# A decoder layer on one core: the causal mask of the maximum as TensorE matmuls, one VectorE reduction over two banks, and a bank of its own for rope

## The reference

```python
# attention: 16 heads of 8, keys and values from a normalised 32-wide latent, rope on q and k, causal
q = (x @ W_q).reshape(b, t, 16, 8).transpose(0, 2, 1, 3)
lat = layernorm(x @ W_dkv) * gamma + beta
k, v = heads(lat @ W_uk), heads(lat @ W_uv)
scores = einsum("bhqd,bhkd->bhqk", rope(q), rope(k)) / sqrt(8)
attn = softmax(where(causal, scores, -inf))
x = x + (attn @ v).reshape(b, t, 128) @ W_o
# cross-attention over 32 context rows: 8 heads of 64, softmax, output projection and bias
# feed-forward 128 -> 352 -> 128: silu(gate) * up, with inputs and weights of every product
# rounded to FP4 in blocks of 16 (scale = max(abs) / 6)
```

## Time and profile before

| | before |
|---|---|
| median of 3 runs, us | 447.8 (447.5 to 450.05) |
| profiled execution, own time / its span, us | 448.12 / 446.4 |
| mean granted clock | 0.75 |
| TensorE busy (matmul) | 300.2 us, 67% |
| VectorE busy | 306.3 us, 69% |
| ScalarE busy | 173.5 us, 39% |
| GpSimd busy | 201.2 us, 45% |
| L821, fused maximum, 256 of them | 114.3 us busy, 49.9 idle before |
| L1069, fills, 256 matmuls | 43.5 us busy, 69.0 idle before |

### The profile page before, as it was taken

How to read it: one execution, slowest core, us unless ns; L and a number is a source line. 1 busy time by engine, 2 the same in 40 slices (tenths; PEclk the granted TensorE clock), 3 DMA queues, 4 the chain that set the end, 5 groups by cost and what they waited for, 6 DMA issues and landing times.

```text
span 446.4 us, 6519 instructions
## 1 busy us (share of the span) xinstructions
PE 300.2 (67%) x1790; PEld 145.2 (33%) x1790; DVE 306.3 (69%) x1136; ACT 173.5 (39%) x326; POOL 201.2 (45%) x376
## 2 busy tenths in 40 slices
PE   0441475877876867869877768596968847567464
PEld 0220142323223222224443324244333314345243
DVE  5742876665575567677788787878778554786972
ACT  1140154565545465243545443444435423222210
POOL 8400033742133444444475644445354661745563
PEclk9995555768788579575969686778859679865796
DMA  6019400025030034003002320030000000000000
GB/s 179 0 61 224 118 0 1 3 100 117 0 73 1 2 121 95 0 1 78 1 8 71 100 50 7 1 76 2 9 1 7 8 1 7 6 1 7 1 12 18
DMA packets 20836, 17.50 MB, mean 39 GB/s; under 512 B 1921, under 2 KB 20225, under 8 KB 20801
## 3 DMA queue, kind: packets, MB, share of 16 engines
q1 hardware_dynamic: 20272, 16.50, 14.8%
q10 hardware_dynamic: 528, 0.59, 0.4%
HBM read 9.62 MB, written 7.34 MB: 38 GB/s over the span
## 4 chain that ended last, share of the span: by engine, by line
PE 45%; DVE 27%; issue 10%; ACT 6%; POOL 6%; DMA 3%; SPq 1%; POOLq 0%; DVEq 0%; ACTq 0%
PE pvp L1104 10%; PE mxp L1069 6%; DVE summed L821 5%; PE st L1093 5%; PE misc L1183 3%; ACT probs L624 2%; PE pvp L1115 2%; PE misc L1165 2%; DVE space L755 2%; PE misc L1168 2%; PE misc L1140 2%; DVE space L752 2%; POOL space L461 2%; DVE xn L735 2%; PE mxp L1004 2%
## 5 line engine op out<-in xcount | busy, mean ns | idle before, releaser
L821 DVE CUSTOM_DVE_ANT_0 summed<-mxp,causal 128x512 bf16<-128x512 f32 (+3 forms) x256 | 114.3, 485 | 49.9 <-PE mxp L1069 49.0
L624 ACT ACTIVATE probs<-st 128x1024 f32<-128x1024 f32 (+1 forms) x96 | 84.5, 880 | 115.6 <-PE st L1093 115.4
L1069 PE MATMUL mxp<-ks,qs 48*128 48x512 bf16 (+3 forms) x256 | 43.5, 377 | 69.0 <-DVE rmax L821 50.4
L1104 PE MATMUL pvp<-probs,va 128*32 128x128 f32 (+3 forms) x512 | 62.5, 565 | 5.1 <-POOL probs L431 5.1
L431 POOL TENSOR_SCALAR_AFFINE_SELECT probs<-probs 128x256 f32<-128x256 f32 x128 | 48.0, 411 | 33.0 <-ACT probs L624 33.0
L1093 PE MATMUL st<-qs,ks 50*128 50x512 bf16 (+3 forms) x256 | 42.3, 371 | 8.2 <-ACT probs L624 6.2
L1069 PEld LDWEIGHTS mxp<-ks,qs 48*128 48x128 bf16 x256 | 12.2, 99 | 92.8 <-DVE rmax L821 44.5
L534 ACT ACTIVATE space<-misc 128x128 f32<-128x128 f32 (+3 forms) x78 | 24.2, 327 | 39.6 <-PE misc L1124 20.2
L422 POOL TENSOR_SCALAR var<-mv 128x1 f32<-128x1 f32 (+1 forms) x36 | 8.9, 248 | 56.9 <-DVE mv L728 55.6
L1093 PEld LDWEIGHTS st<-qs,ks 50*128 50x128 bf16 x256 | 12.1, 101 | 62.4 <-issue 41.5
L461 POOL TENSOR_TENSOR space<-space 128x128 f32<-128x128 f32 (+2 forms) x33 | 24.7, 747 | 15.3 <-DVE space L758 15.3
(11 more groups left out here) (196 smaller groups left out, 587.8 us busy)
## 6 DMA issues: line engine op xcount, KB each, us to landing
parts_dram<-parts SPq DMA_DIRECT2D x8, 384.0 KB, 2.6
qs<-parts_dram SPq DMA_DIRECT2D x16, 192.0 KB, 3.8
ks<-parts_dram SPq DMA_DIRECT2D x16, 192.0 KB, 4.2
parts_dram<-parts SPq DMA_DIRECT2D x8, 256.0 KB, 2.9
xin<-in_x SPq DMA_DIRECT2D x4, 256.0 KB, 6.0
parts_dram<-parts SPq DMA_DIRECT2D x8, 128.0 KB, 2.7
out<-outr SPq DMA_DIRECT2D x16, 64.0 KB, 1.5
qs<-nrows SPq DMA_DIRECT2D x32, 4.0 KB
```

The source lines that it names most:

```text
L624: nc.scalar.activation(probs[n % 2][:, 2 * pair:2 * pair + 2, 512 * k:512 * k + w], st2[:, :].rearrange("p (h q) -> p h q", h=2)[:, :, 0:w ...
L821: last = v.tensor_tensor_reduce(out=summed[:, m % 2, e * w:(e + 1) * w], in0=mxp[m % 3][:, e * w:(e + 1) * w], in1=causal[:, S - w:S], sca ...
L1069: last = mm(units[r][:, e * w:(e + 1) * w], qs[rows, c, i * P:(i + 1) * P], ks[rows, c, 0:w], start=True, stop=True)
L1104: last = mm(pvp[32 * i:32 * i + 32, j * P:S], va[:, j, GH * (n % NG) + i, :], probs[n % 2][:, i, OFF[j]:OFF[j] + S - P * j], start=(j == 0 ...
```

## The change

Six larger units take the place of twelve. TensorE puts the unit of row half 0 into bank 4 and that of row half 1 into bank 5, and then adds the causal mask of the diagonal tile into the same banks by matmuls: for the two halves `lo` of the 128 queries, the 64-row identity strip times the mask strip, with the accumulation left open by the score matmul. The mask's lower half needs only its last 64 columns. One tensor_reduce with negate=True reads both banks (up to 1024 elements per partition) and gives the negative maximum of 2 or 4 rows, so the rows of ks are +1 and not -1. Fill and reduction steps are moved; rope, projections, values_in and set-up use bank 6 (`side`, formerly the third bank of the maxima); the transposed rows of maxima use bank 1 (formerly bank 6). In what the diff leaves out, ScalarE and VectorE read `side` where they read misc[0] or banks[MX_BANK] for xnT, lat, latT, va, rope and set-up, TensorE claims SIDE_BANK for the same pieces, VectorE's loop runs over six units, and ScalarE copies the bank to `halves` ahead of its first piece.

```diff
-MX_BANK, PV_BANK = 4, 7
+MX_BANK, SIDE_BANK, PV_BANK = 4, 6, 7
-MAX_STEPS = [((0, 3), (0, 4)), ((0, 5),), ((0, 6),), ((0, 7), (0, 8)), ((0, 9),), ((0, 10), (0, 11)), (), (),
-             ((1, 0), (1, 1)), ((1, 2),)]
-PAIR_STEPS = [((0, 2),), (), ((0, 3),), ((0, 4),), (), ((0, 5),), (), (), ((1, 0),), ((1, 1),)]
+MAX_STEPS = [(0, 2), None, (0, 3), (0, 4), None, (0, 5), None, (1, 0), None, (1, 1)]
+FILL_STEPS = [(0, 2), (0, 3), None, (0, 4), (0, 5), None, (1, 0), None, (1, 1), None]
-MAX_UNITS = [(3, 0, 0, 1), (3, 1, 0, 1), (3, 0, 1, 1), (3, 1, 1, 1), (2, 0, 0, 1), (2, 1, 0, 1), (2, 0, 1, 1),
-             (2, 1, 1, 1), (1, 0, 0, 2), (1, 1, 0, 2), (0, 0, 0, 2), (0, 1, 0, 2)]
+MAX_UNITS = [(3, 0, 1), (3, 1, 1), (2, 0, 1), (2, 1, 1), (1, 0, 2), (0, 0, 2)]
+NUNIT = len(MAX_UNITS)
...
-        mxp = [pb(f"mxp{i}") for i in range(3)]
+        mx2 = pb("mx2", 1024)
+        mxp = [mx2[:, 0:512], mx2[:, 512:1024]]
         pvp = pb("pvp")
-        misc = [pb(f"misc{i}") for i in range(2)]
-        banks = misc + stp + mxp + [pvp]
+        misc = [pb(f"misc{i}") for i in range(3)]
+        side = misc[2]
+        banks = misc[0:2] + stp + mxp + [side, pvp]
...
-            g.memset(ks[32:HALF, :, :], -1.0)
-            g.memset(ks[HALF + 32:P, :, :], -1.0).then_inc(s["consts_ready"], 1)
+            g.memset(ks[32:HALF, :, :], 1.0)
+            g.memset(ks[HALF + 32:P, :, :], 1.0).then_inc(s["consts_ready"], 1)
...
             def max_rows(n):
                 act.wait_ge(s["nrows_mm"], n + 1)
                 wait(act, "nrows_placed", 32 * n)
-                copy(nrows[:, :], banks[MX_BANK + 2][0:2 * GH, 0:S // 2].bitcast(bf16)).then_inc(s["nrows_d"], 1)
+                copy(nrows[:, :], misc[1][0:2 * GH, 0:S // 2].bitcast(bf16)).then_inc(s["nrows_d"], 1)
...
-                wait(dve, "rmax_d", 12 * n + m - 1)
-                for e in range(k):
-                    last = v.tensor_tensor_reduce(out=summed[:, m % 2, e * w:(e + 1) * w],
-                                                  in0=mxp[m % 3][:, e * w:(e + 1) * w], in1=causal[:, S - w:S],
-                                                  scale=1.0, scalar=NEG, op0=ALU.add, op1=ALU.max,
-                                                  accum_out=rmax[:, i, r, c + e:c + e + 1])
-                last.then_inc(s["rmax_d"], 1)
+                both = mx2[:, :].rearrange("p (r q) -> p r q", r=2)[:, :, 0:k * w]
+                v.tensor_reduce(nmax[:, i, :, c:c + k], both.rearrange("p r (e w) -> p r e w", e=k), axis=AX.X,
+                                op=ALU.max, negate=True).then_inc(s["nmax_d"], 1)
...
-            def max_pair(n, p):
+            def max_fill(n, m):
...
-                units = [claim(MX_BANK + m % 3, "rmax_d", 12 * n + m + 1) for m in (2 * p, 2 * p + 1)]
+                claim(MX_BANK, "nmax_d", NUNIT * n + m + 1)
+                claim(MX_BANK + 1, "nmax_d", NUNIT * n + m + 1)
                 for e in range(k):
                     c = GH // 2 * g + c0 + e
                     for r in range(2):
                         rows = slice(HALF * r, HALF * r + SPLIT)
-                        last = mm(units[r][:, e * w:(e + 1) * w], qs[rows, c, i * P:(i + 1) * P], ks[rows, c, 0:w],
-                                  start=True, stop=True)
-                        if e == k - 1:
-                            last.then_inc(s["mx_mm"], 1)
+                        mm(mxp[r][:, e * w:(e + 1) * w], qs[rows, c, i * P:(i + 1) * P], ks[rows, c, 0:w],
+                           start=True, stop=False)
+                    for lo in range(2):
+                        for r in range(2):
+                            rows = slice(HALF * r, HALF * r + HALF)
+                            last = mm(mxp[r][:, e * w + i * P + HALF * lo:(e + 1) * w], halves[rows, lo, 0:P],
+                                      halves[rows, lo, P + HALF * lo:2 * P], start=False, stop=(lo == 1))
+                last.then_inc(s["mx_mm"], 1)
...
-                m = claim(MX_BANK + 2, "nrows_d", n + 1)[0:2 * GH, 0:S // 2].bitcast(bf16)
+                m = claim(1, "nrows_d", n + 1)[0:2 * GH, 0:S // 2].bitcast(bf16)
...
             pe.wait_ge(s["consts_ready"], 2)
+            m = claim(SIDE_BANK, "halves_d", 1)
+            for lo in range(2):
+                pick = identb[:, HALF * lo:HALF * lo + HALF]
+                for r in range(2):
+                    last = mm(m[HALF * r:HALF * r + HALF, 2 * P * lo:2 * P * lo + 2 * P], pick, squares[:, :],
+                              start=True, stop=True)
+            last.then_inc(s["halves_mm"], 1)
...
-            for p in range(6):
-                max_pair(0, p)
+            for m in range(NUNIT):
+                max_fill(0, m)
             max_rows(0)
-            for p in range(2):
-                max_pair(1, p)
+            for m in range(2):
+                max_fill(1, m)
```

More of the change, by code:

```diff
@@ L414, in _ @@
                                 pattern=[[-1, P]], channel_multiplier=1)
-            g.affine_select(out=causal[:, S - P:S], in_=causal[:, S - P:S], compare_op=ALU.is_ge, fill=NEG, base=0,
+            g.affine_select(out=causal[:, :], in_=causal[:, :], compare_op=ALU.is_ge, fill=NEG, base=0,
                             pattern=[[-1, P]], channel_multiplier=1)
@@ L563, in project @@
                     wait(act, "v_mm", b)
-                    nc.scalar.activation(latT[0:LAT, :], misc[0][0:LAT, :], ACT.Identity, bias=beta[:, :],
+                    nc.scalar.activation(latT[0:LAT, :], side[0:LAT, :], ACT.Identity, bias=beta[:, :],
                                          scale=gamma[:, :]).then_inc(s["latT_d"], 1)
[L566 to L572, removed]
+                for which in range(2):
+                    if (g, u) == WHEN[f"swap{which}"]:
+                        act.wait_ge(s["cos_d"], 2 * b + which + 1)
+                        wait(act, "low_d", 2 * b + which - 1)
+                        copy(turned[0:P // 2, which, 1, :], side[P // 2:P, :])
+                        copy(turned[P // 2:P, which, 1, :], side[0:P // 2, :]).then_inc(s["swapped_d"], 1)
                 if (g, u) == WHEN["high0"]:
@@ L687, in _ @@
             act.wait_ge(s["consts_ready"], 2)
+            act.wait_ge(s["halves_mm"], 1)
+            copy(halves[:, :, :].rearrange("p e q -> p (e q)"), side[:, :]).then_inc(s["halves_d"], 1)
             for name in ("xnT", "lat", "swap0", "latT", "high0", "swap1", "mid0", "high1", "mid1"):
@@ L758, in round_fp4, with turn_cos @@
                 v.scalar_tensor_tensor(norm, norm, BIT_DOWN, expo, ALU.mult, ALU.add).then_inc(s[sum_name], 1)
-            def turn_cos(b, side):
-                n = 2 * b + side
+            def turn_cos(b, which):
+                n = 2 * b + which
                 dve.wait_ge(s["rope_mm"], n + 1)
                 wait(dve, "low_d", n - 1)
-                v.tensor_tensor(turned[:, side, 0, :], banks[MX_BANK][:, :], cos[:, :], ALU.mult)\
+                v.tensor_tensor(turned[:, which, 0, :], side[:, :], cos[:, :], ALU.mult)\
                     .then_inc(s["cos_d"], 1)
@@ L960, in _ @@
                         set_up(n, u)
-                    for ahead, m in MAX_STEPS[u]:
-                        if in_range(n + 1 + ahead):
-                            max_unit(n + 1 + ahead, m)
+                    if MAX_STEPS[u] and in_range(n + 1 + MAX_STEPS[u][0]):
+                        max_unit(n + 1 + MAX_STEPS[u][0], MAX_STEPS[u][1])
         @block.tensor
@@ L1215, in _ @@
                         set_up(SET_UP.index((n, u)))
-                    for ahead, p in PAIR_STEPS[u]:
-                        if in_range(n + 1 + ahead):
-                            max_pair(n + 1 + ahead, p)
+                    if FILL_STEPS[u] and in_range(n + 1 + FILL_STEPS[u][0]):
+                        max_fill(n + 1 + FILL_STEPS[u][0], FILL_STEPS[u][1])
                     if in_range(n - 1):
```

48 lines of the change are left out of this document (23 added, 25 removed).

## The result

The changed kernel takes 473.1 us (median of 4 runs, 471.8 to 475.2) against 448.1 before: a ratio of 1.056, interval 1.050 to 1.061, so +25 us where +16.4 was forecast. Medians are over all runs of a kernel, ratios and their intervals leave out those that came out slow (in a slower state or over 1.5% above the kernel's fastest), so the two can differ a little.

The account below looks back on a forecast made before the run. No engine is full; TensorE and VectorE hand work back and forth, so the chain bounds the kernel. Start 3.5, late slots 10, light slots 2.5 and side bank 0.4 add 16.4 us to 448.1: 464.5 us, range 450 to 478.

Parts of the forecast that it names:

- Start: Before the loop, six fills and reductions no longer overlap: 11.8 us instead of 8.3, +3.5 us.
- VectorE's work: Per slot, plain reductions cost 6.2 us against 6.6 for the fused instructions: a gain of 0.4 us.
- Masks: TensorE's mask matmuls: eight blocks per slot, 0.11 us each at full clock and 0.16 at half, 0.9 to 1.3 us.
- Late slots: Slots 5 to 14: +1.0 us each along the chain, bounds -0.3 to +2.3, together +10 us.
- Step (e): Late slot: fill (0, 5), now at u4, waits for reduction (0, 4), +0.2 us, and its own masks +0.2.
- rival 1: Denser TensorE work keeps the granted clock up in late slots: -3.0 us per slot, 434.5 us if all ten; chance 0.11.
- Light slots: Slots 0 to 4, where scores and exponentials alternate: +0.5 us each, +2.5 together, bounds 0 and +1.5 each.
- (b): Behind L746, reduction (1, 1) takes 1.22 us where one of 0.62 + 0.09 released the fill before: +0.5 us.
- (c): The masks of fills (0, 2) and (0, 3) run at half clock on the path: +0.3 us.
- Side bank: Rope frees the fills, -0.6 x 3; values wait in slots 4 and 8, +0.85 each; set-up +0.5; net +0.4 us.
- The rows of maxima on bank 1: Transposes wait 0.7 us for L907, the bank's last reader, but hidden: 0; uncovered it would be 0.5 us.
- Tail: After the last maximum, a change of more than 1 us would show the prediction wrong.

Follow-up runs that it names:

- e4: The kernel before with only its masks moved to TensorE and plain one-bank reductions, three banks kept: 452.7 us, ratio 1.005.
- e5: e4 without the mask matmuls, so the maximum is over unmasked scores: 443.7 us, ratio 0.994 to the kernel before.
- e7: e4 with every mask matmul issued twice: 456.8 us, ratio 1.023 to the kernel before.
- e2: The changed kernel with two TensorE fills later, (0, 3) at u2 and (0, 5) at u5: 462.9 us, ratio 1.030 to the kernel before.
- e11: e5 with two banks for the maxima in place of three, nothing else changed: 479.5 us, ratio 1.078 to the kernel before.
- e6: e2 with the values' projection and set-up pieces back on bank 0: 458.8 us, ratio 1.026 to the kernel before.
- e8: The kernel before with rope moved to bank 1 and the fills and reductions for (1, ...) units at earlier steps: 450.5 us, ratio 1.005.
- e1: The changed kernel without its mask matmuls, everything else kept: 476.2 us, ratio 1.061 to the kernel before.
- e10: e6 without its mask matmuls: 453.0 us, ratio 1.019 to the kernel before.
- e12: e5 with the moved steps and rope bank of e8: 453.2 us, no interval.

## Why the prediction was right where it was, and where not

The direction, the range (450 to 478) and the mechanism held: both banks in one unit make the fills wait, VectorE's saving is small, TensorE's masks are cheap. The size was 9 us low, mostly by one term (5), and one other (4) is right in its sum by luck. Of the terms:

1. *Start*, +3.5: measured +3.4, and 53.32 against the 53.4 given. The fills ran at the 0.61 us counted for half clock, whatever the clock row says.
2. *VectorE's work*: reductions as computed. The busy sum of the group fell from 135.3 us (114.3 and 21.0 of reads) to 99.4, but the engine's only by 12.4, since the reads had overlapped their neighbours; the prediction's 0.4 a slot makes 6.4. What the other 6 are wasn't taken apart.
3. *Masks*: each block is 0.09 to 0.11 us on the chain at full clock and 0.16 to 0.17 at half, against 0.11 and 0.16. e4 against e5 makes it 5 us, e7 against e4 8 us for the whole set. The Trainium skill (TensorE: Matmul & The Clock Gate, Part 3) says that a weight load overlaps matmuls in flight only where the row group differs. By the prediction's estimate from it, 1.7 us a slot, the masks would have cost 27 us more; neither run shows that.
4. *Late slots*, ten times +1.0: measured +8.0 and +2.2 over the ten pieces, +10.2. The sum is right by luck, the shape isn't: the first five lose 1.6 each, the last four next to nothing. Step (e), the wait of the fill (0, 5) at u4 for the reduction before it, was given 0.2 us; by the timeline it is 0.99, 0.69, 0, 0.40 and 0.40 in the first five and 0.17 in the last five. The rest of the first five's loss isn't taken apart; e2, which moves the fill (0, 3) too, takes 6.2 us of it back. At the end the higher clock stands on the other side: over the last four pieces it is 0.82, against 0.77 before. That is rival 1 in a small part; that the clock is the reason for the even last slots is argued, not shown, since the moved steps and the joined reduction may do it too (see e11).
5. *Light slots*, five times +0.5: **this is the term that failed**, +9.4 measured against +2.5, and over its own upper bound of 5 times 1.5. The prediction carried only steps (b) and (c) over. Step (e) was priced by its cover, L1165 and L1129 in front of the fill, which are row work and don't exist before slot 5; nor does row work stand in front of the fill (0, 3) at u1. The two reductions are bare on the chain there (0.97 and 1.24 us with 0.14 of release each), and the fill (0, 5) waited 1.41 us in each of slots 2, 3 and 4. In those three slots the excess is 2.4, 2.2 and 2.6 us. e4, with the masks on three banks, loses 1.7 us over the five pieces, so the masks explain little of it. e2 takes 2.1 us back. Whether the side bank (term 6) is part of it stays open, for the reason given at e6.
6. *Side bank*, +0.4 net: e6 gives 2 to 4 us for its losing half, 2.2 predicted, with overlapping intervals. The half that gains (rope off the maxima's bank) wasn't run by itself; with the moved steps it gains nothing (e8). The rows of maxima on bank 1 were put at 0: TensorE waited there for L905 for 1.9 us in all, in five slots.
7. *Tail*: +0.7, within the 1 us named.

Of the signs that the prediction set, a late slot came to 21.7 us on average where 21.6 was given. One sign of being wrong, a mean clock well over 0.75, seems to have come with 0.83. Most of that is the unrecorded start; over the late slots the clock is 0.77 and 0.82 against 0.74 and 0.77 before, a small rise. A slip in the chances changes nothing: as listed they add up to 0.09 within 1% and 0.81 slower, where 0.11 and 0.79 were given.

Left without a run of its own is the part of the joined reduction against two of one bank each with everything else equal; e1 against e11 (1.061, 1.078) holds it together with the steps and the side bank.

## What to carry to other kernels

Count buffers before instructions: one PSUM bank fewer between two engines that take turns cost 37 us here with identical work (e11), while 512 extra short matmuls cost 5 to 8. Price a moved step in every phase of the kernel, since what covers it in one phase may not exist in another. Before going after a long wait, look whether the engine behind it has room: twice here the waits were halved and no time was gained.

## What the runs showed that had not been expected

- A fused reduction's read of the accumulator (0.08 us, 256 of them, 21 us in the group view) overlaps its predecessor: the next instruction starts 0.62 us after a start whose own duration is 0.69. Group sums overstate such pairs.
- The mean granted clock of a whole profile differed by 0.06 between executions of e5 of like time (443.4 us at 0.755, 442.1 at 0.813). In the profiles here the start up to 70 us is recorded at 0.5 in three (before, e10, e12) and at 1.0 in ten, while its matmuls last as long. Compare clocks over a later stretch, or check them against the length of a known matmul.
- Fewer matmuls can go with a lower granted clock: 0.79 to 0.72 in e1, with no time gained. It isn't the rule: 0.78 to 0.76 in e5, 0.76 to 0.77 in e10.
- The runs of one kernel scatter by up to 2% where the steps of the engines are in near balance (e4: 445.7 to 454.2 in ten runs), so differences under 1% are left open.
